# A counting stage on one core: the zeros of an accumulator written by ScalarE instead of opened and closed by TensorE

## What is computed

```python
def _gin_conv(x, src, dst, W1, b1, W2, b2):
    agg = jax.ops.segment_sum(x[src], dst, num_segments=N_NODES)
    h = x + agg
    h = jnp.maximum(h @ W1 + b1, 0.0)
    return h @ W2 + b2
```

## Time and profile before

| what | value |
|---|---|
| median of 3 runs | 6454.86 us (6450.83 to 6454.93) |
| the profiled execution's own time | 6452.62 us |
| its span, first to last instruction | 6451.0 us |
| mean granted TensorE clock over the span | 0.836 |
| counting stage, first chunk to last | about 158 to 996 us of the span |

### The profile page before, as it was taken

How to read it: one execution, slowest core, us unless ns; L and a number is a source line. 1 busy time by engine, 2 the same in 40 slices (tenths; PEclk the granted TensorE clock), 3 DMA queues, 4 the chain that set the end, 5 groups by cost and what they waited for, 6 DMA issues and landing times. The chain is left out here.

```text
span 6451.0 us, 102509 instructions
## 1 busy us (share of the span) xinstructions
PE 4280.7 (66%) x26702; PEld 2996.7 (46%) x26703; DVE 3790.3 (59%) x8560; ACT 1190.6 (18%) x1987; POOL 3581.8 (56%) x3658
## 2 busy tenths in 40 slices
PE   0666667385277777776366666663877778787884
PEld 0111114263156566665255555552545556565663
DVE  8777772154589899998466666665111235555553
ACT  0111111112211111111211122111211222222221
POOL 1222224502377777774277777760666667777772
PEclk9999999797589999998577766666988888988886
DMA  4000004200244444443233333335122222222233
GB/s 191 12 15 14 12 15 182 63 21 30 72 127 116 124 117 123 123 118 83 75 82 81 80 81 81 81 62 187 56 65 61 69 67 76 76 78 75 77 76 42
DMA packets 332968, 513.66 MB, mean 80 GB/s; under 512 B 104565, under 2 KB 245919, under 8 KB 322966
## 3 DMA queue, kind: packets, MB, share of 16 engines
q0 software_dynamic: 130656, 290.33, 17.9%
q1 hardware_dynamic: 202166, 221.78, 10.7%
HBM read 409.97 MB, written 101.86 MB: 79 GB/s over the span
## 5 line engine op out<-in xcount | busy, mean ns | idle before, releaser
L1027 POOL DMA_INDIRECT e_ring<-att_rows,e_near x1792 | 1839.6, 1027 | 550.3 <-issue 483.3
L1094 PE MATMUL e_psum<-e_ring,e_whole_pick 128*128 128x264 f32 (+1 forms) x3584 | 870.2, 397 | 301.7 <-DVE e_ring L1254 293.1
L1785 POOL DMA_INDIRECT e_nodes<-x,e_edges x832 | 814.6, 979 | 282.5 <-issue 263.0
L1094 PEld LDWEIGHTS e_psum<-e_ring,e_whole_pick 128*128 128x128 f32 x3584 | 667.7, 231 | 427.2 <-issue 192.1
L1049 PE MATMUL e_px<-t_parts,e_pick 128*128 x5376 | 700.4, 273 | 108.8 <-DVE e_pick L1156 51.5
L1172 DVE TENSOR_TENSOR e_prod<-e_px,e_ring 128x512 f32<-128x512 f32 x672 | 458.1, 682 | 486.3 <-DMA e_ring<-att_rows,e_near 390.5
L285 PE MATMUL b_acc<-b_pick_key,b_pick_lo 128*128 128x416 bf16 (+1 forms) x1960 | 498.1, 341 | 168.8 <-DVE b_pick_key L256 150.7
L1049 PEld LDWEIGHTS e_px<-t_parts,e_pick 128*128 128x128 bf16 x5376 | 459.3, 109 | 201.4 <-issue 130.5
L1701 POOL DMA_INDIRECT sorted<-rx_held,rx_index x432 | 425.3, 984 | 220.5 <-issue 210.4
L355 PE MATMUL r_pa<-gru_counts,gru_parts 128*128 x3000 | 449.6, 316 | 134.8 <-DMA r_bh<-in_gru_bh 95.8
L1136 ACT ACTIVATE e_whole_pick<-e_pturn 128x512 f32<-128x512 bf16 x448 | 266.6, 595 | 1324.8 <-PE e_pturn L1085 1297.9
(11 more groups left out here) (336 smaller groups left out, 6306.4 us busy)
## 6 DMA issues: line engine op xcount, KB each, us to landing
e_relb<-place SPq DMA_DIRECT2D x56, 1024.0 KB
e_ring<-att_rows,e_near POOLq DMA_INDIRECT x1792
sorted<-o_fill SPq DMA_DIRECT2D x11, 2508.0 KB
e_edges<-sorted SPq DMA_DIRECT2D x209, 132.0 KB
kept<-gin_counts SPq DMA_DIRECT2D x5, 4000.0 KB, 35.3
gru_counts<-kept SPq DMA_DIRECT2D x5, 4000.0 KB
rx_held<-in_edge_rows POOLq DMA_DIRECT2D x52, 297.0 KB
e_nodes<-x,e_edges POOLq DMA_INDIRECT x832
```

Of the source, the lines that this page charges most:

```text
L1027: pool.indirect_dma_start(out=ring[:, s, r, 0:wd + HEADS], out_offset=None, in_=xrows, in_offset=bass.IndirectOffsetOnAxis(ap=near[:, s, r ...
L1094: mm = pe.matmul(psum[q % 2][:, 0:RING], whole_pick[:, q % 2, c, :], ring[:, s, q * G + c, :], start=(c == 0), stop=(c == G - 1))
L1785: pool.indirect_dma_start(out=nodes[:, s, u, :], out_offset=None, in_=source, in_offset=bass.IndirectOffsetOnAxis(ap=edges[:, q, u, RBF + ...
```

## The change

ACT takes over the zeros. Before the loop it writes zeros to all four banks (an `activation` with function Copy from the `zeros` tile to PSUM), and behind each eviction it writes zeros to the pair that it has just moved out, once its own moves have completed; each such write raises `blank`. PE waits for `blank` where it waited for `moved`, and its four zero matmuls per window go; a single semaphore increment (`opened`, for which nobody waits) stands in their place. The matmuls of the chunks carry `start=False, stop=True`. With `closed` gone, ACT reads the window's last step from `bounds` into a register, and waits until `used` has reached the count of all chunks up to it. POOL's threshold on `moved` falls by 2, since ACT no longer raises it at the start.

```diff
--- before.py
+++ after.py
@@ -178,8 +178,8 @@
         zeros = m.sb("b_zeros", [P, BANK], BF16)
         sender = Sender(m, D, "b", *COUNT_SENDS)
         acc = [m.ps(f"b_acc{s}", [P, 2, BANK]) for s in range(2)]
-        loaded, ready, picked, used, closed, moved, diag = (
-            m.sem(f"b_{n}") for n in ("loaded", "ready", "picked", "used", "closed", "moved", "diag"))
+        loaded, ready, picked, used, blank, opened, moved, diag = (
+            m.sem(f"b_{n}") for n in ("loaded", "ready", "picked", "used", "blank", "opened", "moved", "diag"))
         halves = ((0, 0, KEYS_L), (1, KEYS_L, KEYS))
         real = slice(2 * NWIN, 2 * NWIN + NC)
         flat = AT[:, :, :].rearrange("p j d -> p (j d)")
@@ -204,7 +204,7 @@
                 sender.begin(pool)
 
                 def add_own(t):
-                    pool.wait_ge(moved, t * (2 * PER) + 2 * PER + 2)
+                    pool.wait_ge(moved, t * (2 * PER) + 2 * PER)
                     block_ = flat[:, ds(t * (NP + P), P)]
                     pool.tensor_tensor(block_, block_, K["identb"][:, :], ALU.add).then_inc(diag, 1)
                 sender.send(pool, 0, 0, first=True)
@@ -258,14 +258,21 @@
 
             @block.scalar
             def _(act):
-                act.sem_inc(moved, 2)
+                act.wait_ge(used, 2)
+                for s in range(2):
+                    for h, lo, hi in halves:
+                        act.activation(acc[s][:, h, 0:hi - lo], zeros[:, 0:hi - lo], ACT.Copy).then_inc(blank, 1)
                 with act.Fori(0, NT) as t:
                     for q in range(PER):
-                        act.wait_ge(closed, t * PER + q + 1)
+                        last = act.value_load(K["bounds"][0:1, ds(t * PER + q + 1, 1)], min_val=1, max_val=NSTEP + NWIN)
+                        act.wait_ge(used, last * 2 + 2)
                         for h, lo, hi in halves:
                             act.activation(AT[:, lo // WIN:hi // WIN, ds(t * P + q * WIN, WIN)],
                                            acc[q % 2][:, h, 0:hi - lo].rearrange("p (j d) -> p j d", d=WIN),
                                            ACT.Copy).then_inc(moved, 1)
+                        act.wait_ge(moved, t * (2 * PER) + q * 2 + 2)
+                        for h, lo, hi in halves:
+                            act.activation(acc[q % 2][:, h, 0:hi - lo], zeros[:, 0:hi - lo], ACT.Copy).then_inc(blank, 1)
 
             @block.tensor
             def _(pe):
@@ -274,21 +281,15 @@
                     for q in range(PER):
                         w = pe.snap(t * PER + q)
                         lo, hi = bounds(pe, w)
-                        pe.wait_ge(moved, w * 2)
-                        for h, a, z in halves:
-                            pe.matmul(acc[q % 2][:, h, 0:z - a], zeros[:, 0:P], zeros[:, 0:z - a],
-                                      start=True, stop=False, skip_group_check=True)
+                        pe.wait_ge(blank, w * 2 + 2)
+                        pe.sem_inc(opened, 1)
                         with pe.Fori(lo, hi) as n:
                             for b in range(2):
                                 pe.wait_ge(picked, n * 2 + b + 1)
                                 for h, a, z in halves:
                                     mm = pe.matmul(acc[q % 2][:, h, 0:z - a], pick_lo[:, b, :], pick_key[:, b, a:z],
-                                                   start=False, stop=False, skip_group_check=True)
+                                                   start=False, stop=True, skip_group_check=True)
                                 mm.then_inc(used, 1)
-                        for h, a, z in halves:
-                            mm = pe.matmul(acc[q % 2][:, h, 0:z - a], zeros[:, 0:P], zeros[:, 0:z - a],
-                                           start=False, stop=True, skip_group_check=True)
-                        mm.then_inc(closed, 1)
 
 
 class Split:
```

## The result

The changed kernel takes 6525.4 us (median of 4 runs, 6514.3 to 6533.8) against 6454.9 us, a ratio of 1.011 with an interval of 1.0097 to 1.0122: 70 us or 1.1% slower. It was forecast slower, at 6500 us in a range of 6462 to 6530. The profiled execution is the slowest of the four, 6533.8 us (span 6532.2 us), 81 us above that of before; the next phase's first DMA starts at 1077.71 instead of 1000.39, so that 77 of the 81 us lie in the counting stage.

What follows compares the result with a forecast made beforehand. DVE and PE taking turns at two buffers bound the counting stage; across boundaries, DVE's register work, then PE's openings. 6452.6 plus 52, less 3.5, less 4, plus 1 gave 6498.1, forecast as 6500 us, range 6462 to 6530.

Steps and rivals of the forecast that it cites:

- part 7: At counting-stage window boundaries, PE's emptier gaps bring the low clock at 65 of 99, 0.8 us each: 52 us.
- A: The clock holds in the counting stage and the first chunk waits for `pick_key` alone; likeliest 6448 us; chance 0.12.
- Rival B: Only some window boundaries of the counting stage, 20 to 45, get a low-clock spell; 6472 us; chance 0.14.
- D: PE waits for ACT's zeros in the counting stage; each us would cost 100 us; chance 0.01.
- Rival C: A low-clock spell at every window boundary at full price, 99 x 1.0 us; 6559 us; chance 0.08.
- Part 3: At boundaries PE waits for `blank` and issues a lone increment instead of openings; 0.04 us gained each, 4 us in all.
- the 18 us of the upper bound: The most gained at all boundaries without PE's openings, if the increment is free.
- the loop's head: PE's work at a window's start that ran beside the openings and now comes in the open; taken as 0.24 us.
- Parts 4 and 5: ACT's zero writes cost 0; ACT leaves windows 0.35 us sooner; next phase's first DMA 0 to 1 us later: 1 us.
- What would show it: Signs in the counting stage: 838 to about 883 us, PEclk 0.99 to about 0.87, low spells behind short boundaries too.
- part 2: At a window's start, without openings, the first chunk could start when `pick_key` is ready; at most 18 us in all.

Runs made afterwards that it cites:

- zeros_back: The changed kernel with four zero matmuls per window put back on PE, into a spare bank, two behind the increment and two behind the last chunk: 6460.4 us, ratio 1.0012.

## Why the prediction was right, and where it was off

- **The mechanism (part 7) is shown.** The clock fell at most boundaries, short ones included, and putting the four matmuls back restored it with everything else of the change in place. The rival on the other side (A) needed the clock to heed something else or not to heed zeros; zeros_back rules out both. Rival B's 20 to 45 spells were passed. D fell too: ACT's zeros are done 5.8 us or more before PE's chunks, except in the last window. The gaps came as forecast: 1.52 us on average at short boundaries and 2.10 at long ones, against 1.54 and about 2.1.
- **The size of part 7 was off, in errors against each other.** I took two boundaries in three, a choice that no row gave; it was 96 of 99, so nearly the upper bound. And I took each spell at 3.41 us, as the four of before lasted; more than a quarter of the 85 unbroken ones last longer, up to 17.1 us inside the stage, so that low time came to 453 us and not 65 x 3.41 = 222. Against that, 0.8 us for 3.41 us is 0.23 per us, and the runs give 0.18. My 52 us for new spells should have been 453 x 0.18 = 80. That is why the forecast of 6500 lies 25 us under the median of 6525.4. That the median lies inside the range is partly luck, since too little low time and too high a price cancel in part: the 453 us at my price would have been 106 us and a time of some 6554, outside it.
- **What the rows could have told.** The price: 0.33 us more for a round of 1.74 is 0.19 per us, and 3.41 us hold two such rounds, not two and a half. The length they couldn't: no row of before shows a low stretch that meets the next boundary. That slower rounds, with fewer matmuls in the same time, are what holds the clock down is argued only: no run here takes the two apart.
- **What PE did before a spell was read wrongly.** I wrote that two openings came before each of the four. In three of the four (191.84, 328.37, 635.57) the clock fell, by the trace's clock records, while PE was still idle, 0.04 to 0.13 us before the openings, which then ran slowly; only at 912.05 had openings and chunks gone before. So three of the four falls came out of the gap itself:

```profile
191.88 0.85 PE L279 MATMUL b_acc<-b_zeros 128*128 128x416 bf16 x2 [1.41 <-ACT gin_counts L266]
```

- **Rival C's 6559 us** had nearly the right count, but at 1.0 us each where 80 / 96 = 0.83 us is what came. The range reached 6530, and of the four runs one lies just below this edge (6529.2) and one above it (6533.8): it was too narrow upwards.
- **Part 3 (the increment) held.** I put PE at 346.58 against 346.62 and took 0.04 us per boundary. At boundaries without a spell DVE's second round takes 1.549 us at the 37 short ones and 1.649 at 13 long ones, where it took 1.570 and 1.677: 0.02 to 0.03 us. Of the 18 us of the upper bound the increment eats some 12: with a small filler in its place 0.12 us per boundary come back, 99 x 0.12. The rest, the loop's head by my sum, no run takes apart.
- **Parts 4 and 5 held.** The next phase's first DMA starts 3.45 us after ACT's last eviction begins (1077.71 - 1074.26; 1000.39 - 996.97 = 3.42 before):

```profile
1074.26 0.90 ACT L270 ACTIVATE gin_counts<-b_acc 128x416 f32 x2 [0.98 <-PE b_acc L290]
1075.19 0.93 ACT L275 ACTIVATE b_acc<-b_zeros 128x416 f32<-128x416 bf16 x2
...
1077.71 0.38 SPq L315 DMA_DIRECT2D g_hid<-in_x  x1
```

- **What would show it** came out in kind: PEclk lower (0.75, forecast 0.87), the stage longer (915 us, forecast 883), low spells behind short boundaries too. At short boundaries DVE's second round stayed at 1.55 us (1.57 before), which I had called the sign that the increment eats part 2. Other stages are about 4 us apart, which is more than the 2 us that I allowed and one of my signs of being wrong; executions of the changed kernel alone differ by up to 20 us, so it tells nothing here.

## What to carry to other kernels

Before taking "useless" matmuls off PE, look at what the clock does where they stand: a few spells at 0.50 in a stage say that its load may be just enough, and then a few matmuls less can bring the low clock at nearly every boundary. The price is that of the rounds, not of the matmuls: here 0.18 us for each us at the low clock, since a chunk's matmul took 533 ns there instead of 355 but DVE's `pick_key` 491 as against 490. If work must go from such a place, put cheap filler matmuls into a spare bank where PE waits for its sequencer anyway, and count how long that wait is, since a filler too many stands in the way of real work. And at the head of a short loop, register loads can be the longest item: one load less on DVE and PE was worth more here than all the rest.

## What was unexpected in the hardware

- A low spell can run on through a whole window of chunks: with gaps of 1.5 to 2.1 us, one in each window of some 9 us, the clock stayed low for up to 17.1 us at a stretch, though PE had chunks all the while (the row 418.30:435.40 has 36 matmuls in 17.1 us). "TensorE: Matmul & The Clock Gate" of the Trainium skill, "A second HAM failure mode", speaks of an engine that swings between its two levels when groups of matmuls cycle through PSUM. The changed kernel agrees, with half of 915 us at the lower one; but the kernel before cycles through the same banks and had 14 us of it, so the cycling alone doesn't decide.
- A stage that was within four spells of full clock was at half clock for half of its time after losing 4 of some 24 matmuls per window.
- One register load with its sums costs DVE 0.62 us (idle time 1.31 to 0.69), twice what the load alone shows.
